# Scaled values written as bf16 ahead of the fp8 clamp, and the output bank handed back by its first reader

## The reference, cut to what matters

```python
def _div_clamp_fp8(x, scale):
    y = jnp.clip(x.astype(jnp.float32) / scale, -FP8_MAX, FP8_MAX)   # FP8_MAX = 448
    y = y.astype(jnp.bfloat16).astype(jnp.float32)
    return _fp8_roundtrip(y)
...
q, k = _ln(linear(ln_out, wq)), _ln(linear(ln_out, wk)); v = linear(ln_out, wv)      # fp8 linears
core = _gqa(q, k, v)                       # 16 heads of 128, 8 kv heads, softmax
xout = _gqa(qx, kx, vx)                    # the same against ctx
catq = _div_clamp_fp8(concatenate([core, xout]), proj_smooth)
return einsum(catq, wproj) * (proj_in_scale * proj_w_scale)
```

## Time and profile before

| | us |
|---|---|
| median of 3 runs (lowest, highest) | 1618.06 (1617.77, 1619.49) |
| the profiled execution's own time | 1618.53 |
| its span, first to last instruction | 1616.7 |
| block 3's unit pipeline in it | about 311 to 786 |

### The profile page before, as it was taken

One profiled execution on the slowest core, in us unless ns is written; L12 is line 12 of the kernel. 1 busy time (PEld: TensorE's weight loads), 2 busy tenths in 40 slices (PEclk: granted clock), 3 DMA queues, 4 the chain that ended last, 5 costly groups with the idle time before them and its releaser, 6 DMA issues.

```text
span 1616.7 us, 26814 instructions
## 1 busy us (share of the span) xinstructions
PE 1275.2 (79%) x9052; PEld 921.2 (57%) x9108; DVE 1194.5 (74%) x2669; ACT 974.1 (60%) x2887; POOL 291.0 (18%) x369
## 2 busy tenths in 40 slices
PE   5774666579799798799689999657676777998898
PEld 4663344256566566576567777334444444886686
DVE  4786789869989999987434541889898998784353
ACT  2562486688778688687245651358788888332221
POOL 0000222234344354353100000000101000001000
PEclk7995677589999999999989999868798989996999
DMA  5301000100000000000520000000000000100000
GB/s 221 143 4 66 39 0 0 56 1 5 4 1 7 0 1 7 0 1 1 194 81 1 1 1 1 20 1 1 1 0 0 0 1 1 52 0 1 1 1 26
DMA packets 13583, 38.12 MB, mean 24 GB/s; under 512 B 2201, under 2 KB 8866, under 8 KB 10802
## 3 DMA queue, kind: packets, MB, share of 16 engines
q1 hardware_dynamic: 13490, 36.99, 6.0%
HBM read 35.94 MB, written 1.05 MB: 23 GB/s over the span
## 4 chain that ended last, share of the span: by engine, by line
DVE 41%; PE 38%; issue 10%; ACT 8%; POOL 1%; another core or an unknown queue 0%; DVEq 0%; DMA 0%; SPq 0%; ACTq 0%; POOLq 0%
DVE small L2507 7%; DVE work L2517 4%; PE PS L3084 4%; DVE work L1188 2%; PE PS L1917 2%; PE PS L1842 2%; PE PS L1401 2%; PE PS L1948 2%; DVE work L1238 2%; DVE small L1222 2%; DVE work L1200 2%; ACT work L1383 1%; PE PS L368 1%; DVE work L1187 1%; PE PS L1409 1%
## 5 line engine op out<-in xcount | busy, mean ns | idle before, releaser
L2423 ACT ACTIVATE work<-PS,small 128x1024 f32<-128x1024 f32 x128 | 154.5, 1207 | 20.1 <-DVE small L2509 14.5
L2507 DVE TENSOR_REDUCE small<-PS 128x1 f32<-128x1024 f32 x128 | 155.6, 1216 | 4.8 <-PE PS L2334 3.9
L1292 POOL TENSOR_TENSOR small<-small,minus_half 128x4 f32<-128x4 f32 x96 | 108.6, 1131 | 255.0 <-ACT small L1333 254.9
L1409 PE MATMUL PS<-late 128*128 128x512 f16 x384 | 105.0, 401 | 51.4 <-DVE work L1216 45.0
L2354 PE MATMUL PS<-ident_b,work 128*128 128x128 bf16 x1024 | 91.5, 241 | 66.6 <-DVE work L2517 53.3
L1383 ACT ACTIVATE work<-PS,small 128x128 f32<-128x128 f32 x256 | 90.3, 365 | 53.9 <-DVE small L1223 53.8
L213 POOL TENSOR_TENSOR rstd<-moments,eps 128x1 f32<-128x1 f32 x56 | 13.8, 246 | 586.8 <-DVE moments L193 586.8
L2354 PEld LDWEIGHTS PS<-ident_b,work 128*128 128x128 bf16 x1024 | 67.1, 108 | 77.6 <-DVE work L2517 52.3
L2517 DVE TENSOR_SCALAR work<-work 128x1024 bf16<-128x1024 f32 x128 | 87.6, 684 | 13.1 <-ACT work L2423 11.0
L1409 PEld LDWEIGHTS PS<-late 128*128 128x128 f16 x384 | 35.8, 100 | 106.0 <-DVE work L1216 55.9
L2416 ACT COPY work<-PS 128x512 f32<-128x512 f32 x128 | 74.9, 585 | 31.4 <-PE PS L2354 30.9
(11 more groups left out here) (416 smaller groups left out, 3433.9 us busy)
## 6 DMA issues: line engine op xcount, KB each, us to landing
late<-in_C_proj SPq DMA_DIRECT2D x1, 4096.0 KB, 12.2
ctxT<-in_ctxT SPq DMA_DIRECT2D x24, 128.0 KB, 2.6
late<-in_C_q SPq DMA_DIRECT2D x1, 2048.0 KB, 8.1
late<-in_C_qx SPq DMA_DIRECT2D x1, 2048.0 KB, 12.6
late<-in_F_w SPq DMA_DIRECT2D x2, 1024.0 KB
late<-in_B_gate SPq DMA_DIRECT2D x1, 1024.0 KB, 8.3
late<-in_B_up SPq DMA_DIRECT2D x1, 1024.0 KB, 10.1
late<-in_B_down SPq DMA_DIRECT2D x1, 1024.0 KB, 12.1
```

The costliest lines, as they stand in the source:

```text
L1292: return nc.gpsimd.tensor_tensor(rs, rs, minus_half[:, 0:4], ALU.pow)
L1409: last = nc.tensor.matmul(PS[:, n, :], src(k), w, start=k == 0 and part == 0, stop=k == KC - 1 and part == 1)
L2423: nc.scalar.activation(E_[g]["e"], banks(g, 2), ACT.Exp, scale=small[:, g, h:h + 1], bias=small[:, g, 48 + h:49 + h], accum_out=small[:, g ...
L2507: ch.link(nc.vector.tensor_reduce(small[:, g, 80:81], banks(g, 2), AX.X, ALU.max))
```

## The change

Three edits, all in block 3. In rounded, L1238 writes the scaled values into y (bf16) and no longer into t (f32), and the clamp L1239 works in place on y. In activations, L1200 writes y_in (bf16) and the clamp L1203 works in place on it. L1238 now counts on a new flag C_oread (which shares the semaphore of an older flag, B_qturned), VectorE itself waits for that count ahead of the clamp, and weigh(u) on TensorE waits for C_oread(u-1) in place of C_shifted(u-1). C_shifted is kept for GpSimd.

```diff
-        B_qturned = flag("B_qturned")
+        B_qturned = flag("B_qturned_C_oread")
...
+        C_oread = follow(B_qturned, ROUNDS)
...
-                    last = nc.vector.tensor_scalar(c["t_in"][:, k * P:(k + 1) * P], xT[:, k, g, :], inv[:, n * KC + k:n * KC + k + 1],
+                    last = nc.vector.tensor_scalar(c["y_in"][:, k * P:(k + 1) * P], xT[:, k, g, :], inv[:, n * KC + k:n * KC + k + 1],
                                                    448.0, ALU.mult, ALU.min)
                 ch.link(last)
-                ch.link(nc.vector.tensor_scalar(c["y_in"], c["t_in"], -448.0, None, ALU.max))
+                ch.link(nc.vector.tensor_scalar(c["y_in"], c["y_in"], -448.0, None, ALU.max))
...
-                ch.link(nc.vector.tensor_tensor(c["t"], heads4(OBANK), over_head(inv[:, 8 + 4 * r:12 + 4 * r]), ALU.mult))
-                ch.link(nc.vector.tensor_scalar(c["y"], c["t"], 448.0, -448.0, ALU.min, ALU.max))
+                nc.vector.tensor_tensor(c["y"], heads4(OBANK), over_head(inv[:, 8 + 4 * r:12 + 4 * r]), ALU.mult).then_inc(C_oread.sem, 1)
+                dve.wait_ge(C_oread.sem, C_oread.nth(i, u))
+                ch.link(nc.vector.tensor_scalar(c["y"], c["y"], 448.0, -448.0, ALU.min, ALU.max))
                 fp8_shift(ch, c["y"], c["m"], c["t"]).then_inc(C_shifted.sem, 1)
...
-                    pe.wait_ge(C_shifted.sem, C_shifted.nth(i, u - 1))
+                    pe.wait_ge(C_oread.sem, C_oread.nth(i, u - 1))
```

## The result

The changed kernel takes 1609.01 us (median of 14 executions, 1600.85 to 1617.86) against 1619.96 us for the kernel before on the same chip (14, 1616.38 to 1628.24). The ratio is 0.9922 with a 95% interval of 0.9907 to 0.9938, which is 12.6 us less, between 10.0 and 15.1. It goes with the means of the executions, which lie 12.5 us apart; the two medians lie 10.95 us apart. The profiled execution took 1606.58 us, its span is 1604.8.

What follows compares the result with a forecast made beforehand. VectorE was taken to bound the slots with inputs, TensorE later ones. Three periods 5.1 us, fill 0.7 and 0.4, last ring 0.6, drain 2.1: 8.9 us off 1618.06, 1609.2 us; range 1605.0 to 1613.8.

Steps and rivals of the forecast that it cites:

- stays at 427: Rival: the 512-column clamp gets no faster in place, leaving drain and earlier weigh, 3.5 us, 1614.6 us; chance 0.06.
- The slower rival: Rival: each unit pays the register's arithmetic for VectorE's new wait; at 0.2 us a unit about 1622 us; chance 0.04.
- slots of the first kind: Three of a period's 16 slots: L1188 comes earlier, L1292 and L1303 follow, full 0.20 us gained, 0.6 us a period.
- slots of the second kind: Four slots a period: earlier VectorE loses as much cover as it gains; only 66 ns behind GpSimd's hold count, 0.27 us.
- the q ring: L1216, project_q, squares, L1292, next L1216: does not shorten; where it ends last, clamp time saved is only waited out.
- The stretch from 474 to 508: Part of each period: 0.4 us from clamps and earlier weigh, 0.3 from two clamps behind, together 0.7 us.
- the exponentials' ring: VectorE's wait for ScalarE's exponentials, 12.4 us; shortens with the change, two clamps in it giving 0.3 us a period.
- The stretch from 455 to 474: Part of each period where TensorE is busy and VectorE has slack: gains nothing.
- Fill and last ring: Block 3 up to 388: 0.7 and 0.4 us; ring of exponentials from 727 to 774, four or five clamps: 0.6 us.
- The drain: End of block 3: last weigh begins 1.95 us earlier, and with its own clamp the drain is 2.1 us shorter.
- the hold absorbs the saving: Rival: L1303's hold and the power's ring keep slots in place; only input clamps and drain gain, 1613.9 us; chance 0.17.
- VectorE bounds throughout: Rival: all 10.6 us of clamps paid, plus drain and freed half microseconds, 14 us less, 1604 us; chance 0.10.

Runs made afterwards that it cites:

- regwait_only: Kernel before, with VectorE waiting for L1238 by the flag worked out from the loop's register instead of the constant link; ratio 0.9991.
- in_clamp: Kernel before with both bf16 edits (input activations and 512-column clamp), constant link and weigh's old wait kept; ratio 0.9954.
- wait_only: Kernel before with only weigh's wait moved to the bank's first reader, L1238, which still writes f32; ratio 0.9983, 1616.92 us.
- in_only: Kernel before with only the input activations writing bf16 ahead of their clamp; ratio 0.9984, 1618.64 us.
- the half pair: Kernel before and changed kernel, each with GpSimd's subtraction on two of four heads only; 1604.79 and 1592.58 us, one execution each.
- clamp_twice: Changed kernel with the 512-column clamp in rounded issued twice; ratio 1.0024 to the kernel before, 1623.14 us.
- q_first: Changed kernel with normed_q ahead of the input activations in VectorE's order; ratio 0.9870 to the kernel before, 1602.83 us.
- largest_first: Changed kernel with largest ahead of rounded in VectorE's order; ratio 1.0399 to the kernel before, 1684.30 us.

## Why the prediction was right

**The durations.** All four held: the clamps at 297 and 227 ns (forecast 294 and 228), L1239 at 683 ns, L1201 at 0.47 us for a pair that is not held. The time for which L1201 is held did grow, which the prediction had as a sign of being wrong, by 2.0 us in all and not by the 10.6 us that the clamps gave: 0.35 us in each of three slots like the one at 403, and 0.9 us in the slot at 556, where a fall of the clock had kept L1303 behind the pair in the profile before. The clamp that "stays at 427" is out.

**The register's wait.** No wider gap ahead of the clamp, and regwait_only at 0.9991. The slower rival wanted more than 0.14 us a unit; it is out.

**Where GpSimd's power moves with L1188.** In slots of the first kind the size is right, 0.21 us a slot for 0.20, but not the way to it. The prediction had L1188 come earlier and "L1292 and L1303 follow". L1292 did not follow: it starts 3.46 us after L1217 as before, and is shortened, because less of L1188 lies beside it. So this gain has an end. Once no overlap is left, at 1.01 us, a shorter clamp moves nothing there; 0.20 us of it are left now. For slots of the second kind it was mis-sized: the prediction let L1303 stand "where the q ring puts it" and counted 66 ns a slot, 0.27 us for the four. In three of the four L1292 is lengthened by L1188 as well (1.35 us before, 1.21 or 1.13 after), they gained 0.20 or 0.21 each, and only the slot at 403, whose power runs alone at 1.01 us, behaves as forecast and worse: 8.04 to 8.19. Together the four gave 0.46 us a period. The generalisation came from the one slot that stood in the earlier trace rows, which was the exception.

**The stretch from 474 to 508.** Forecast 0.7 us, measured 34.64 to 34.17, 0.47. The clamps in the exponentials' ring gave 0.37 of it; the first part, clamps and the earlier weigh together, was mis-sized, 0.10 us for 0.4. All of the 0.10 is the clamps': in_clamp, with the old wait, has these slots at the same lengths, and wait_only has them as before. ScalarE's L1378 was next in line at the scores, and the prediction looked only to VectorE there. So the terms of a period that the prediction counted sum to 0.63 + 0.46 + 0.14 + 0.47 = 1.70 us, the 1.7 of the forecast, by two errors that cancel, which is luck. The stretch from 455 to 474, held at nothing, gained too: its first two slots are 0.06 us shorter each where the clock stays up (6.70 to 6.64, 6.23 to 6.17). The rest of the three periods' 5.4 us is balance of slots in which the clock fell.

**Fill and last ring.** 1.7 and 1.5 us for 1.1 and 0.6: both forecasts look low, but much of it lies in the profile of the kernel before. There TensorE's clock came up later in the fill (granted 0.75 from 326 to 345, against 0.91 in the same stretch of the changed kernel, 330.1 to 349.1), and at 757.9 L1303 held L1223 for 0.78 us. regwait_only, whose VectorE has the same work as the kernel before, has the fill at 74.2 and the last ring at 45.05 us; against these the change gives 0.5 and 0.8 us. With 5.5 us for the clean periods and 2.1 for the drain that is an estimate of 9.0 us for block 3, where the pair of profiles has 10.7.

**The drain.** 2.15 us for 2.1, by the steps forecast: counted from its start, the last weigh begins 1.95 us earlier. In both profiles the matmul groups of the drain kept their 1.03 to 1.10 us, which those of in_only and regwait_only did not.

**The rivals.** That the hold absorbs the saving is refuted by the slots and by the half pair, 10.4 against 10.7 us. That VectorE bounds throughout would be 14 us in block 3. It holds in most slots with inputs, which pay the whole 0.20 us, and fails in the slot at 403 and from 455 on; clamp_twice pays 73% in all. The times alone do not refute it: the measured 12.6 us (10.0 to 15.1) lies between it and the forecast's 8.9, which is outside that interval, so it was nearer than its chance of 0.10 said. The time of 1609.01 met 1609.2 so closely by luck: the kernel before ran at 1619.96 this time and not at 1618.06, and the saving was larger than forecast by about as much. Besides block 3's 10.7 us the profiles differ by 1.2 us outside it, where nothing was changed. Of the 12.6 us, the edits measured apart give 10.2 (7.5 for in_clamp, 2.8 for wait_only); the rest, 2.4 us, is left open, as is the 0.24% that came with the register's wait. The 512-column clamp's share was the most off, 4.3 us forecast and 5.7 measured alone.

## What to carry to other kernels

For a saving on an engine that two rings share with a helper engine, list the period slot by slot and ask in each what started the helper's instruction and whether the shortened instruction lies beside it; one slot of each kind is not enough. When a freed wait is counted, look past the next engine for every producer that the following instructions read, since the first one late takes the gain back. A hold between VectorE and GpSimd can be made cheaper by placing work that reads PSUM where the hold falls, as q_first does; part of it then falls on what stands behind that work. Before a stage is moved ahead, its own inputs' arrival in the slot has to be read first, as largest_first shows.

## What the runs showed of the hardware

- GpSimd's small power (128x4) is stretched by a VectorE L1188 (SBUF alone, f32 out) that started before it: 1.01 us alone and 1.35 us with 0.49 us of overlap, 1.21 with 0.34, 1.13 with 0.27, always the overlap less 0.14 us. Where the power started first, VectorE took its usual time beside it (0.29 us for L1187 at 478, 0.69 to 0.73 us for L1188). GpSimd's subtraction does the opposite: VectorE's L1201, on f32 with a scalar from SBUF, stood still, and so did L1224 on four columns (0.17 to 0.62 us).
- VectorE writes bf16 from an f32 PSUM source in the time of f32, 683 and 684 ns for 512 columns; the step behind it is what gets faster, 427 to 297 ns.
- After 2.5 us of waiting, TensorE did the next 1.04 us of work in 1.89 us, and such a slot was 0.65 us longer. Executions of one kernel spread over 17 us (1600.85 to 1617.86), and one profile could hide a saving of 2 us (wait_only's drain). Two kernels can be compared slot by slot in single profiles, where the granted clock is the same in both.
